# At least one tile per expert, and six weight pieces split between the expert tiles

## What is computed

```python
x = x + tanh(g_xattn) * xattn(layernorm(x), ctx_512, Wq, Wkv_expand, Wout)   # 16 heads of 32, 64 keys
x = x + tanh(g_ffn) * ffn(layernorm(x), gate_w, w1, w2, w3, ws1, ws2, ws3)

def ffn(x):                      # E = 8 experts, K = 2, inner size 256, one shared expert
    scores = softmax(xf @ gate_w.T)
    weights, idx = top_k(scores, 2)
    h = einsum('td,eid->eti', xf, w1)
    g = silu(h) * einsum('td,eid->eti', xf, w3)
    eo = einsum('eti,edi->etd', g, w2)
    y = einsum('etd,te->td', eo, comb)           # comb: the two weights of a token, else 0
    z = silu(xf @ ws1.T) * (xf @ ws3.T) @ ws2.T  # shared expert
    return y + z
```

## Time and profile before

| what | value |
|---|---|
| median of 3 runs | 525.67 us (522.79 to 526.62) |
| the profiled execution: its time | 521.47 us |
| its span | 519.7 us |
| PE busy | 436.1 us (84%) |
| DVE busy | 318.6 us (61%) |
| ACT busy | 245.8 us (47%) |
| POOL busy | 245.0 us (47%) |
| mean granted TensorE clock | 0.947 of full |

### The profile page before, as it was taken

How to read it: one execution, slowest core, us unless ns; L and a number is a source line. 1 busy time by engine, 2 the same in 40 slices (tenths; PEclk the granted TensorE clock), 3 DMA queues, 4 the chain that set the end, 5 groups by cost and what they waited for, 6 DMA issues and landing times. The chain is left out here.

```text
span 519.7 us, 8145 instructions
## 1 busy us (share of the span) xinstructions
PE 436.1 (84%) x2432; PEld 232.6 (45%) x2433; DVE 318.6 (61%) x641; ACT 245.8 (47%) x425; POOL 245.0 (47%) x209
## 2 busy tenths in 40 slices
PE   2699599988999889987867625999999999999991
PEld 1355355554555545553333202455455545445540
DVE  4798868987588865897988761433433334343330
ACT  4878644663356534485746320343344343434430
POOL 4008325405544154465687813255555555455432
PEclk9999989999999999998978855999999999999997
DMA  8970001120011100325747664266576575655653
GB/s 327 412 304 1 0 1 42 42 81 2 1 64 38 61 0 0 108 116 182 244 121 241 165 122 102 41 109 113 104 121 109 99 119 102 123 105 110 108 75 42
DMA packets 26375, 55.31 MB, mean 106 GB/s; under 512 B 9136, under 2 KB 9264, under 8 KB 25712
## 3 DMA queue, kind: packets, MB, share of 16 engines
q0 software_dynamic: 9760, 20.49, 22.3%
q1 hardware_dynamic: 16592, 34.54, 20.2%
HBM read 31.51 MB, written 23.50 MB: 106 GB/s over the span
## 5 line engine op out<-in xcount | busy, mean ns | idle before, releaser
L1293 PE MATMUL bank<-arena 128*128 128x512 f16 (+1 forms) x576 | 109.5, 347 | 3.2 <-issue 1.5
L1293 PE MATMUL bank<-arena,GT 128*128 x468 | 109.6, 385 | 0.1
L526 POOL DMA_INDIRECT out<-Y,entry x39 | 61.6, 1579 | 84.4 <-ACT Y L792 39.0
L1293 PE MATMUL bank<-arena,gT 128*128 (+1 forms) x330 | 84.1, 393 | 6.3 <-DVE gT L815 5.8
L1293 PEld LDWEIGHTS bank<-arena 128*128 128x128 f16 x576 | 55.9, 98 | 51.4 <-issue 3.8
L541 ACT ACTIVATE arena<-bank 128x512 f16<-128x512 f32 (+1 forms) x88 | 49.7, 586 | 52.5 <-PE bank L1293 32.3
L1293 PEld LDWEIGHTS bank<-arena,GT 128*128 128x128 f16 x468 | 46.3, 99 | 48.5 <-issue 3.1
L815 DVE TENSOR_TENSOR GT<-bank,GT 128x512 f16<-128x512 f32 x39 | 27.0, 692 | 61.0 <-ACT GT L541 61.0
L453 POOL TENSOR_TENSOR arena<-arena,rd 128x1024 f32<-128x1024 f32 x16 | 30.5, 1905 | 52.3 <-DVE rd L928 52.3
L1293 PEld LDWEIGHTS bank<-arena,gT 128*128 128x128 f16 x330 | 32.7, 100 | 44.7 <-DVE gT L815 5.8
L1293 PE MATMUL bank<-arena,x2T 128*128 128x512 f16 x192 | 47.9, 403 | 4.4 <-DVE x2T L815 4.4
(11 more groups left out here) (126 smaller groups left out, 596.2 us busy)
## 6 DMA issues: line engine op xcount, KB each, us to landing
x_sb<-in_experts SPq DMA_DIRECT2D x16, 768.0 KB, 6.1
xrows<-xn SPq DMA_DIRECT2D x16, 256.0 KB, 2.2
out<-x_sb SPq DMA_DIRECT2D x16, 256.0 KB, 2.1
xrows<-Y SPq DMA_DIRECT2D x1, 2304.0 KB, 23.9
out<-Y SPq DMA_DIRECT2D x1, 2304.0 KB, 28.8
x_sb<-in_x SPq DMA_DIRECT2D x2, 1024.0 KB, 7.8
x_sb<-in_x SPq DMA_DIRECT2D x1, 2048.0 KB, 15.8
arena<-in_wq SPq DMA_DIRECT2D x1, 1024.0 KB, 8.0
```

The costliest lines, as they stand in the source:

```text
L526: nc.gpsimd.indirect_dma_start(out=out, out_offset=bass.IndirectOffsetOnAxis(ap=entry[:, j, 0:1], axis=0), in_=Y[:, j % RING, :], in_offse ...
L1293: last = nc.tensor.matmul(dst, a, b, start=n == 0, stop=n == len(steps) - 1)
```

## The change

Four things.

1. The pieces 10 to 15 are split at the end of the expert steps of tiles 0 to 5, one each (AT_STEP), the high part by ScalarE behind Y, the low part by VectorE behind the gating. For j < 8 TensorE's `hidden_e(j)` waits for pieces 2j and 2j + 1; its other waits for weights go. Rounds 0 to 2 (FIRST_ROUNDS) are written out, so that these steps can differ, and the Fori covers 9 rounds.
2. In `tile_table` a count is at least 128, so each expert gets at least one tile, and tile j can't belong to an expert above j.
3. GpSimd splits none of the pieces from 6 on (LO_BY_POOL); in the last feed-forward ScalarE and VectorE split 6, 7, 8 and 9.
4. SyncE loads 4 to 9, stores the xn2 rows, loads 10 to 12, stores base tiles 0 and 1, loads 13, stores base tiles 2 and 3; pieces 14 and 15 are loaded when tiles 0 and 1 have landed in `out`.

```diff
--- before.py
+++ after.py
@@ -271,7 +271,9 @@
 
         PIECES = 2 * E
         PARTS = 4
-        LO_BY_POOL = (0, 1, 2, 4, 6, 8, 9, 11)
+        LO_BY_POOL = (0, 1, 2, 4)
+        AT_STEP = {0: 10, 1: 11, 2: 12, 3: 13, 4: 14, 5: 15}
+        FIRST_ROUNDS = -(-E // RING)
         ROUTE2 = 9
         PLACED = (ROUTE2 - 1, ROUTE2)
         CONSTS = 15
@@ -353,12 +355,12 @@
             load_pieces(2, 4)
             store_base(B - 2, 1, PER)
             sp.wait_ge(st_base, 16 * PER * (B - 1))
-            load_pieces(4, 12)
+            load_pieces(4, 10)
             store_rows(B - 1)
-            load_pieces(12, 15)
-            store_base(B - 1, 0, 1)
-            load_pieces(15, PIECES)
-            store_base(B - 1, 1, PER)
+            load_pieces(10, 13)
+            store_base(B - 1, 0, 2)
+            load_pieces(13, 14)
+            store_base(B - 1, 2, PER)
 
 
             sp.wait_ge(table_ready, 1)
@@ -378,6 +380,8 @@
             for j in range(TILES):
                 sp.wait_ge(added[j % RING], 16 * (j // RING + 1))
                 sp.sem_inc(landed, 1)
+                if j < 2:
+                    load_pieces(14 + j, 15 + j)
                 if j + AHEAD < TILES:
                     load_list(j + AHEAD)
 
@@ -496,11 +500,7 @@
             with pool.Fori(1, B - 1) as b:
                 iteration(b, b - 1, True)
             iteration(B - 1, B - 2, False)
-            split_piece(6)
-            split_piece(8)
-            split_piece(9)
             scatter_pairs(B - 1)
-            split_piece(11)
 
 
             def gather(j):
@@ -672,24 +672,21 @@
                 c = f + 1
                 turn_hi(c, "x2", 0)
                 turn_hi(c, "x2", 1)
-                split_piece(8)
                 tanh_h(f, 0)
                 turn_hi(c, "x2", 2)
                 turn_hi(c, "x2", 3)
                 router_exp(f)
-                split_piece(9)
+                split_piece(6)
                 tanh_h(f, 1)
                 turn_hi(c, "g", 0)
-                split_piece(10)
-                split_piece(11)
+                split_piece(7)
                 tanh_h(f, 2)
                 turn_hi(c, "g", 1)
-                split_piece(12)
+                split_piece(8)
                 tanh_h(f, 3)
                 turn_hi(c, "g", 2)
-                split_piece(13)
                 turn_hi(c, "g", 3)
-                split_piece(14)
+                split_piece(9)
 
             def probabilities_hi(b, i):
                 turn_hi(b, "p", 2 * i)
@@ -725,7 +722,7 @@
                     scores_out(b + 1, 2)
                     exps(b + 1, 1)
                 else:
-                    for k in range(3, 8):
+                    for k in range(3, 6):
                         split_piece(k)
 
             def project_hi(b, g):
@@ -792,14 +789,16 @@
                 nc.scalar.activation(Y[:, s, :], e_y[s][:, :], ACT.Copy,
                                      scale=entry[:, bass.ds(j, 1), 1:2].rearrange("p n c -> p (n c)").bitcast(F32)
                                      ).then_inc(ey_ready, 1)
-
-            split_piece(15)
+                if isinstance(j, int) and j in AT_STEP:
+                    split_piece(AT_STEP[j])
+
             rows_hi(0, 0)
             rows_hi(1, 1)
             tanh_e(0, 0)
-            for s in range(RING):
-                step(0, s)
-            with act.Fori(1, ROUNDS - 1) as it:
+            for it in range(FIRST_ROUNDS):
+                for s in range(RING):
+                    step(it, s)
+            with act.Fori(FIRST_ROUNDS, ROUNDS - 1) as it:
                 for s in range(RING):
                     step(it, s)
             for s in range(RING):
@@ -1107,7 +1106,7 @@
 
                 dve.wait_ge(pairs_ready, B)
                 link(V.tensor_tensor(count[r, 1, :], count[r, 0, :], list_at[r, :], ALU.subtract))
-                link(V.tensor_scalar(count_i[r, 0, :], count[r, 1, :], float(P - 1), None, ALU.add))
+                link(V.tensor_scalar(count_i[r, 0, :], count[r, 1, :], float(P - 1), float(P), ALU.add, ALU.max))
                 link(V.tensor_scalar(count_i[r, 1, :], count_i[r, 0, :], 7, None, ALU.arith_shift_right))
                 link(V.tensor_copy(count[r, 2, :], count_i[r, 1, :]))
                 link(V.memset(count[r, 3, :], 1.0))
@@ -1130,7 +1129,6 @@
 
                 c = f + 1
                 after_attention(f)
-                split_piece(7)
                 hidden(f, 0)
                 turn_lo(c, "x2", 2)
                 turn_lo(c, "x2", 3)
@@ -1140,18 +1138,19 @@
                 router_place(f)
                 turn_lo(c, "g", 0)
                 hidden(f, 1)
-                split_piece(10)
+                split_piece(6)
                 hidden(f, 2)
                 turn_lo(c, "g", 1)
+                split_piece(7)
                 tile_table()
                 base(f, 0)
+                hidden(f, 3)
                 turn_lo(c, "g", 2)
-                hidden(f, 3)
+                split_piece(8)
                 base(f, 1)
                 turn_lo(c, "g", 3)
                 base(f, 2)
-                split_piece(12)
-                split_piece(13)
+                split_piece(9)
                 base(f, 3)
 
             def shared_lo_half(h):
@@ -1269,15 +1268,16 @@
                 lo(gT[:, 0, 1], e_g[:, 0:IC * P].rearrange("p (c t) -> p c t", c=IC), gT[:, 0, 0]).then_inc(egT_lo, 1)
                 if nxt:
                     hidden_e(j + 1, (s + 1) % RING)
-
-            split_piece(14)
-            split_piece(15)
+                if isinstance(j, int) and j in AT_STEP:
+                    split_piece(AT_STEP[j])
+
             rows_lo(0, 0)
             rows_lo(1, 1)
             hidden_e(0, 0)
-            for s in range(RING):
-                step(0, s)
-            with dve.Fori(1, ROUNDS - 1) as it:
+            for it in range(FIRST_ROUNDS):
+                for s in range(RING):
+                    step(it, s)
+            with dve.Fori(FIRST_ROUNDS, ROUNDS - 1) as it:
                 for s in range(RING):
                     step(it, s)
             for s in range(RING):
@@ -1545,6 +1545,9 @@
                 turn(e_turn, G[:, s, :], DC).then_inc(eT_mm, 1)
 
             def hidden_e(j, s, e):
+                if isinstance(j, int) and j < E:
+                    for k in (2 * j, 2 * j + 1):
+                        pe.wait_ge(w_split[w_slot(k)], PARTS * w_round(k))
                 pe.wait_ge(eT_lo, j + 1)
                 product(e_h[s][:, :], [(lambda h, c=c: GT[:, s, h, c, :], lambda h, c=c: w_at(e, h, c))
                                        for c in range(DC)]).then_inc(eh_mm, 1)
@@ -1560,9 +1563,6 @@
                 if not isinstance(j, int) or j > 0:
                     pe.wait_ge(egT_lo, j)
                 turn(e_g, gg[:, s, :], IC).then_inc(egT_mm, 1)
-                if isinstance(j, int) and j == 0:
-                    for k in range(PIECES - 4, PIECES):
-                        pe.wait_ge(w_split[w_slot(k)], PARTS * w_round(k))
                 if nxt:
                     hidden_e(j + 1, (s + 1) % RING, e_next)
                 pe.wait_ge(egT_lo, j + 1)
@@ -1576,13 +1576,12 @@
             turn_rows(0, 0, 0)
             turn_rows(1, 1, 0)
             e = expert_of(0)
-            for k in range(PIECES - 4, PIECES):
-                pe.wait_ge(w_split[w_slot(k)], PARTS * (w_round(k) - 1) + (e + 2) // E * PARTS)
             hidden_e(0, 0, e)
             pe.wait_ge(base_ready, NT)
-            for s in range(RING):
-                step(0, s)
-            with pe.Fori(1, ROUNDS - 1) as it:
+            for it in range(FIRST_ROUNDS):
+                for s in range(RING):
+                    step(it, s)
+            with pe.Fori(FIRST_ROUNDS, ROUNDS - 1) as it:
                 for s in range(RING):
                     step(it, s)
             for s in range(RING):
```

## The result

The changed kernel takes 536.77 us (median of 4 runs, 535.19 to 539.51) against 524.23 us of the kernel before (4 runs, 521.31 to 526.62): ratio 1.0244, 95% interval 1.0197 to 1.0292, that is 12.5 us by the medians: a slowdown clear of the noise, though the interval reaches just below 2%. Its profiled execution took 535.71 us with a span of 533.9 us; before, 521.47 and 519.7.

What follows compares the result with a forecast made beforehand. TensorE was taken to bound the expert loop, 4.54 us a tile. Terms 9.5 + 3.5 + 1.7 - 1.1 - 1.6 = +12.0 on the median 525.67 gave 537.7 us, range 527.5 to 545 (own case 532 to 543).

Steps and rivals of the forecast that it cites:

- The sum: Whole kernel: stalls, tile 7's wait, half clock, unrolling and seam, 9.5 + 3.5 + 1.7 - 1.1 - 1.6 = +12.0 us.
- The stall of 1.9 us, five times: Expert steps of tiles 0 to 4: splits delay gT's low part, so TensorE waits 1.9 us each, +9.5 us.
- Tile 7's wait, +3.5: Behind tile 5 in the expert loop: hidden_e(7) waits for the split of piece 15, +3.5 us.
- Half clock, +1.7: Behind the 3.5 us gap before tile 7's product: a stretch at granted clock 0.50, +1.7 us.
- Unrolling, -1.1: Expert loop: two fewer round beginnings, 0.55 us each, -1.1 us, bounds 0 and -1.4.
- The loads of pieces 14 and 15, cost 0: Expert loop: loads four steps ahead of their splits, longer steps give gathers room; cost 0, at most 6.1 us.
- The seam, -1.6: Ahead of the expert loop: first gather at 310.8 instead of 312.37, -1.6 us; bounds +1.3 and -4.9.
- split 7: Seam, ahead of the first hidden tile: this 2.46 us split leaves VectorE's way, -1.5 us, bounds 0 and -2.46.
- GpSimd's freedom: Seam: without GpSimd's splits beside them, three small VectorE operations get about 0.6 us shorter each, -1.9 us.
- Hidden splits: Rival, expert loop: splits fall into ScalarE's and VectorE's idle time, only -2.7 us remains, 523.0 us; 9 in 100.
- Only tile 7's wait: Rival, expert loop: middle steps have slack, so 3.5 + 1.7 - 2.7 = +2.5 us, 528.2 us; 7 in 100.
- The clock falling after every stall: Rival, expert loop: half clock follows each 1.9 us stall too, +20.5 us, 546.2 us; 12 in 100.

Runs made afterwards that it cites:

- control: The changed kernel, with only GpSimd's loaded count ahead of each add of rows checked against its bounds; 536.66 us, ratio to before 1.0276.
- in_gaps: The changed kernel, with ScalarE's splits of pieces 10 to 15 moved behind gT's high part, VectorE's one step later behind gT's low part; 528.60 us.
- high_only: The changed kernel without VectorE's low parts of pieces 10 to 15; ScalarE's high parts stay and tell TensorE the piece is ready; 529.01 us, one run.
- pair_at_4: The changed kernel, with pieces 14 and 15 both split behind tile 4 and none behind tile 5; 534.04 us, ratio to before 1.0272.
- late_13: The changed kernel, with the load of piece 13 issued behind the first three list loads instead of ahead of them; 534.81 us, ratio 1.0268.
- unrolled_only: The kernel before, with rounds 0 to 2 written out instead of round 0 alone, and TensorE's wait for the last four pieces on constants; 522.46 us.
- no_split_in_loop: The changed kernel without the six splits in the expert loop; loads of pieces 14 and 15 and written-out rounds stay; 523.48 us, ratio to before 1.0048.
- hole_a: The changed kernel, pieces 10 to 13 split around the first rows, 14 and 15 in gaps, loaded behind twelve list loads; one round written out; 521.12 us.
- hole_c: As hole_a, but piece 13 loaded behind three list loads, TensorE's wait for the last four pieces at hidden_e(5), two rounds written out; 517.33 us.
- hole_b: As hole_a, but pieces 13, 14 and 15 all loaded behind the first three list loads; 523.01 us, ratio to before 1.0035.

## Why the prediction was right, point by point

**The sum.** It said +12.0 us. The medians differ by 12.5, the two profiled spans by 14.2. By the spans the loop cost 3.0 us more than the sum has for it (16.6 against 13.6), and the seam gave 0.8 us more (2.4 against 1.6). So the mechanism was right, but that the medians come within 0.5 us of the sum is luck: the two errors partly cancel, and the medians stand nearer to each other than the spans. The control's ratio, 1.0276, is 14.4 us of its 521.04.

**The stall of 1.9 us, five times: right in mechanism, a little short.** Measured 2.07 us each over 4.54, or 10.1 in sum over the same steps before, the fifth of which had a round beginning. TensorE is idle 1.85 to 1.91 us on VectorE's gT. The difference is in the links: 0.10 us from ScalarE's high part to VectorE's start where I took 0.03, and a down-projection 0.16 us behind the end of gT's low part, where I took none. in_gaps shows that the place is the cause, high_only that without VectorE's part 0.5 to 1.3 us of it are left.

**Tile 7's wait, +3.5: right. Half clock, +1.7: right by its number, for a reason that doesn't hold.** The gap was 3.70 us, the matmuls behind it took 1.6 us longer, the step 10.10 us, 5.4 more than before. The clock term was drawn from one gap of 2.08 us with a fall and one of 1.72 without. The same gap of 2.08 us had no fall in six other traces, and pair_at_4 has one of 3.58 without any. A fall behind such a gap was likely (four of five here), not certain. That the gaps of 1.9 us cost no clock was right (none of the five is followed by a stretch at half, nor any in the control, late_13 and pair_at_4), but the rows of before couldn't tell it.

**Unrolling, -1.1: wrong.** Alone it gave -0.2 us in the loop (unrolled_only); in the changed kernel the last 31 distances take 147.99 us instead of 146.81, +1.2. The failed step is the assumption that a round's beginning has a price of its own that goes with their number. Most of the 3.0 us by which the loop exceeds the sum (16.6 against 13.6) is here: 2.3.

**The loads of pieces 14 and 15, cost 0: right for this kernel only.** no_split_in_loop shows 2.2 us of late gathers as soon as the steps are short. The prediction named longer steps as the cover, and pair_at_4's gather bears that out.

**The seam, -1.6: right in sign, 0.8 us short, and for partly other reasons.** From the start of the first scatter of the third image's second choices (264.17 before, 264.30 after) to TensorE's first row transposes I find 51.97 us before and 49.44 after; in the five other kernels with the same order of loads 50.80, 49.01, 49.62, 50.08 and 48.53, so -1.2 to -3.4. VectorE's chain gained more than I wrote: scatters from 281.41 (I said 282.6), the last base sum at 300.19 (302.0). From that first scatter on, the first hidden tile's operation (272.27) came 2.5 us earlier than before, the whole of split 7 and not 1.5 of it, and the scatters another 2.2 us (1.9). The DMA side took back a part: piece 13 landed 7.6 us after its issue instead of 6.1, and the first gather came at 310.16 (310.8). That a piece ahead of the lists costs was right (late_13): the first gather came 2.4 us after the piece landed, 2.7 were predicted.

GpSimd's freedom was worth a little more than the earlier trace rows promised: the mask operation takes 0.19 us in the changed kernel, 0.83 before. The traces show delays the other way round too: beside VectorE's split a scatter issue takes 1.64 us instead of 0.96, in the kernel before (287.30) as in the changed one (282.75), and in the changed one the next (284.69) takes 2.48, beside another split, against 0.96 before. This would fit the interface that GpSimd and VectorE share (the Trainium skill, page "Advanced Engine Details and Errata", section GPSIMD Details); no run isolates it.

**The rivals.** Hidden splits: false where the change puts them, true in in_gaps. The Trainium skill's page "Perfetto Trace Analysis", section Identifying the Most-Contended Engine, calls occupancy a fair measure of how near Vector and Scalar are to their limit. The traces agree as far as in_gaps goes, where the room was there. They show too that it doesn't tell where in the queue the room is: ScalarE and VectorE are about 40% busy in the loop both before and after, and it lost 16.6 us. Only tile 7's wait: false. The clock falling after every stall: false here, as said above.

## What to carry to other kernels

An engine that is 60% idle has room for more work only where its queue has the gap: find the instruction that the bounding engine waits for next, and put the new work behind it, not ahead. Measure the slack of that link first (here 0.74 us against 2.65 of delay). When a load is moved in a queue, ask what small transfer stands behind it; the list entries of 1 KB decided when the loop could start.

## What the runs showed of the hardware that I had not expected

- A gap of 3.58 us on TensorE left the granted clock at 1.00 in one kernel, and gaps of 3.58 to 3.72 us were followed by 0.50 in four others. A gap of 2.08 us before the same work was followed by 0.50 in six of twelve traces.
- The beginning of a round of the engines' loop costs 0.2 to 1.1 us of TensorE's time, and how much differs from program to program: the same loop body had 0.7 us in the kernel before and 1.1 in the changed one at most rounds. The cause is open.
- The first gather of 128 rows landed 3.3 to 4.0 us after its issue with no weight piece or one in flight (before, late_13, in_gaps, pair_at_4, hole_a, hole_c), and after 6.8 us with three (hole_b).
- Where TensorE had a wait at the end of a round, over before its current product ended, its next work still came 1.2 us late (hole_a, and hole_b by its step of 5.95 us); that the wait is the reason isn't shown.
